# Four terms instead of three in the score products of both attentions

## The chip, the cores and the metric

One of the NeuronCores of one Trainium2 chip runs the whole program as one launch. The metric is the device time of the launch in microseconds (us). Engines in the rows: PE is TensorE (PEld its weight loads), DVE VectorE, ACT ScalarE, POOL GpSimd, SP the engine that here only issues DMAs and waits; a "q" behind an engine's name is its DMA issuing.

## The reference, cut to what matters

Two layers over 4096 tokens of 256 features, 16 heads of 16 features. Layer 0: layer norm, then a sparse attention plus an FP8 product. Layer 1: layer norm, then a causal rotary attention plus a block with its own causal attention (with per-head RMS norms) and a mixture of four experts. All in float32. The scores are what the change touches:

```python
# layer 0: keys of the query's own 128-block, and every 8th key (512 in all)
w = jnp.einsum('bhnqd,bhnkd->bhnqk', fq, fk) * scale + fmask
w = jax.nn.softmax(w, axis=-1)
# layer 1, twice: all earlier keys
scores = jnp.einsum('bhqd,bhkd->bhqk', Q, K) / math.sqrt(Dh)
attn = jax.nn.softmax(jnp.where(causal, scores, min), axis=-1)
```

## The kernel before, in words

Stages run one after another, with a wait of every engine for every queue between them: embed (layer 0's norm and projections), sparse attention, middle (layer 1's projections), dense attention (two attentions, one loop), and a last stage with projections and experts. The function `attend` builds both attention stages.

**Number parts.** A float32 query or key is stored in DRAM as two arrays, its high part (rounded to the format that TensorE takes in one pass) and the low rest. `TERMS` (L27) lists the products that make up a score: high with high, high with low, low with high. Each takes 16 rows (`HEAD_DIM`), so the operand tiles hold 48 rows per head (`TROWS`), and behind them two rows (`MROWS`) that hold ones in the keys and the negated row maximum, in two parts, in the queries: 50 rows (`SROWS`) in all. Two heads lie in one tile, an even one from row 0 and an odd one from row 64 (`HALF`); a tile holds two such pairs side by side. Each term's rows are a DMA of their own: for each of the two halves and three terms, 16 rows of two pieces of 2 KB, 64 KB in all.

**Units.** A unit is one group of 4 heads and one strip of 512 queries: 32 units in the sparse stage, 64 in the dense one (8 groups of 8 strips; strips upwards in even groups, downwards in odd ones). For each unit there are
- "tiles" (L852, L859, L863): score products of queries by keys over `TROWS` rows, of which DVE takes row maxima (L1022, L1026, L1029). Some (L871) go by ACT's copies and POOL's running maximum instead;
- "negate" and "hand": DVE negates the maxima, PE turns them (L876), DVE copies them (L1057), and SP writes them by two DMAs into the spare rows of the query tile (L793);
- "unit", then "score" (L902, L911, L921): score products of keys by queries over `SROWS` rows, so that the maximum is already taken off, and ACT's exponential (L965);
- "weigh" (L942): probabilities by values; "out": PE turns the result, DVE divides, SP stores it (L799).

One list, `order`, fixes the sequence for all engines. The tiles run ahead of the scores, by a distance that starts small in the dense stage and grows with the units done.

**Loads.** SP issues, in the list's order: at first the queries of units 0 and 1 (L754), in the sparse stage with their own keys and values (L763, L765), then the strided keys of three groups (L740), and in the dense stage masks and ones. After that the load of unit n+2 stands at the first tile of unit n+1, and the hand-over of a unit stands behind such a load. A sparse unit is 6 DMAs of queries, 6 of keys and 1 of values. A dense unit is 6 of queries, and in the first 8 units 6 of keys of the first group as well (`load_keys`, L727). The keys of the 7 later dense groups are loaded by POOL, 6 DMAs of 512 KB each and one of values of 2 MB, in two buffers; the load for the second group stands at unit 1. PE waits for counts of these DMAs (`count_loaded`, `handed`, `wait_keys`) at the first tile of a unit and at "unit".

Of the kernel before, what the change touches and what calls it, by code (L numbers as in the profile page):

```python
# [16 lines left out]
P = 128  # L17
# [6 lines left out]
GROUP = 4  # L24
GROUPS = HEADS // GROUP
GCOL = 32
TERMS = ((0, 0), (0, 1), (1, 0))  # L27
TROWS = len(TERMS) * HEAD_DIM
MROWS = 2
SROWS = TROWS + MROWS  # L30
HALF = P // 2
PAIRS = GROUP // 2
SCALE = HEAD_DIM ** -0.5
STRIDE = 8
# [45 lines left out]
def _build(nc, ctx, d, out):  # L80
# [461 lines left out]
    def attend(jobs, stage, splits, past):  # L542
# [4 lines left out]
        held = 6 if sparse else 8  # L547

        per_unit = 16 * 15 if sparse else 16 * 8  # L550
        earlier = 0 if sparse else 4 * 16 * 15

        def count_loaded(n):

            if sparse:
                return per_unit * (n // 8) + 16 * 13
            return earlier + per_unit * (n // 8) + 16 * 12

        def handed(n):

# [111 lines left out]
        with ExitStack() as st:  # L672
# [48 lines left out]
            def load_keys(queue, group, tokens, loaded):  # L721
                a, g = groups[group]
                for odd in range(2):
                    for i, (_, part) in enumerate(TERMS):
                        src = parts_d[a][part][DIM + g * GROUP * HEAD_DIM:DIM + (g + 1) * GROUP * HEAD_DIM, tokens]
                        first_row = odd * HALF + i * HEAD_DIM
                        queue.dma_start(keys[group % 2][first_row:first_row + HEAD_DIM, :, tokens].bitcast(F32),  # L727
                                        src.rearrange("(h o e) t -> o e h t", o=2, e=HEAD_DIM)[odd]).then_inc(loaded, 16)

            def load_values(queue, group):  # L730
                a, g = groups[group]
# [2 lines left out]
            def load_strided(queue, g):  # L734

                for odd in range(2):
                    for i, (_, part) in enumerate(TERMS):
                        src = str_d[part][g * GROUP * HEAD_DIM:(g + 1) * GROUP * HEAD_DIM, :]
                        first_row = odd * HALF + i * HEAD_DIM
                        queue.dma_start(str_keys[g][first_row:first_row + HEAD_DIM, :, :].bitcast(F32),  # L740
                                     src.rearrange("(h o e) t -> o e h t", o=2, e=HEAD_DIM)[odd]).then_inc(str_in[g], 16)
                queue.dma_start(str_values[g][:], v_d[0][g].rearrange("(c p e) n -> p c e n", p=P, e=STRIDE)
                             [:, :, STRIDE - 1, :]).then_inc(str_in[g], 16)

            def attend_sp():
                def load_queries(n):
                    a, g, j = units[n]
                    if n >= held:
                        sp.wait_ge(weighed, ends[n - held])
                    for odd in range(2):  # L750
                        for i, (part, _) in enumerate(TERMS):
                            src = parts_d[a][part][g * GROUP * HEAD_DIM:(g + 1) * GROUP * HEAD_DIM, j * STRIP:(j + 1) * STRIP]
                            first_row = odd * HALF + i * HEAD_DIM
                            sp.dma_start(queries[n % held][first_row:first_row + HEAD_DIM, :, :].bitcast(F32),  # L754
                                         src.rearrange("(h o e) t -> o e h t", o=2, e=HEAD_DIM)[odd]).then_inc(queries_in[n % 8], 16)
                    if not sparse and n < STRIPS:
                        load_keys(sp, 0, slice(j * STRIP, (j + 1) * STRIP), queries_in[n % 8])
                    if sparse:
                        for odd in range(2):
                            for i, (_, part) in enumerate(TERMS):  # L760
                                src = parts_d[a][part][DIM + g * GROUP * HEAD_DIM:DIM + (g + 1) * GROUP * HEAD_DIM, j * STRIP:(j + 1) * STRIP]
                                first_row = odd * HALF + i * HEAD_DIM
                                sp.dma_start(keys[n % held][first_row:first_row + HEAD_DIM, :, :].bitcast(F32),  # L763
                                             src.rearrange("(h o e) t -> o e h t", o=2, e=HEAD_DIM)[odd]).then_inc(queries_in[n % 8], 16)
                        sp.dma_start(values[n % held][:], v_d[a][g, j * STRIP:(j + 1) * STRIP, :].rearrange("(b p) n -> p b n", p=P)).then_inc(queries_in[n % 8], 16)  # L765

                def load_split(i):
                    tiles, loaded, chunks = splits
                    src, high, _ = chunks[i]
                    if i >= 2:  # L770
                        sp.wait_ge(split_done, i - 1)
                    sp.dma_start(tiles[i % 2][:, 0:high.shape[1]], src).then_inc(loaded[i % 2], 16)

                load_queries(0)
                load_queries(1)
                if sparse:
                    for g in range(1, GROUPS):
                        load_strided(sp, g)
                else:
                    for tile, name in halves:  # L780
                        load_halves(tile, name, masks_in)
                    for tile in with_ones:
                        load_ones(sp, tile, masks_in)
                for kind, n, what in order:
                    if kind == "queries" and n + 1 < len(units):
                        load_queries(n + 1)
                    elif kind == "unit" and n < len(splits[2]):
                        load_split(n)
                    elif kind == "hand":
                        sp.wait_ge(side_freed, side_at[kind, n, what] + 1)  # L790
                        for odd in range(2):
                            first_row, rows = odd * HALF + TROWS, MROWS * PAIRS * BLOCKS
                            sp.dma_start(queries[n % held][first_row:first_row + MROWS, :, :].bitcast(F32).rearrange("s h (b p) -> s (h b) p", p=P),  # L793
                                         neg_rows[n % 2][odd * rows:(odd + 1) * rows, :].bitcast(F32)).then_inc(queries_in[n % 8], 16)
                    elif kind == "out":
                        a, g, j = units[n]
                        sp.wait_ge(side_freed, side_at[kind, n, what] + 1)
                        cols = slice(g * GROUP * HEAD_DIM, (g + 1) * GROUP * HEAD_DIM)
                        sp.dma_start(rows_of(ao_d[a], j)[:, :, cols], aos[n % 2][:]).then_inc(ao_stored[n % 2], 16)  # L799

            def wait_keys(n):

                group = n // STRIPS
                if group >= 1:
                    pe.wait_ge(keys_in[group % 2], 96 * ((group + 1) // 2))

            def attend_pe():
                def rows(h, n):
# [23 lines left out]
                for kind, n, what in order:  # L832
# [10 lines left out]
                    if kind == "tile":  # L843
                        kc, h, b = what
                        if what == tiles_of(n)[0]:
                            pe.wait_ge(queries_in[n % 8], count_loaded(n))
                            if sparse:
                                pe.wait_ge(str_in[n // STRIPS], 16 * 7)
                            else:
                                wait_keys(n)  # L850
                        if kc == "strided":
# [1270 lines left out]
```

## Time and profile before

| | |
|---|---|
| median of 3 runs | 5109.05 us |
| lowest, highest | 5077.86, 5117.56 us |
| profiled execution, its own time | 5059.35 us |
| its span | 5057.5 us |
| mean granted TensorE clock in it | 0.931 |
| PE, PEld, DVE, ACT, POOL busy | 92%, 50%, 75%, 61%, 30% |

### The profile page before, as it was taken

How to read it: one execution, taken by the hardware profiler on the slowest of the kernel's cores; microseconds unless marked ns; L12 is line 12 of the kernel's file. 1: busy time of each engine (PE TensorE's matmuls, PEld its weight loads, DVE VectorE, ACT ScalarE, POOL GpSimd, SP SyncE). 2: the span in 40 equal slices, each digit the busy share in tenths (PEclk: the TensorE clock that was granted, in tenths of full speed). 3: DMA queues.
4: the chain of work that ended last, by engine and by line, in shares of the span. 5: the costliest groups of instructions: out<-in, count | busy, mean ns of one | idle time of the engine just before them, and what ended most of it. 6: DMA issues, size and time to landing. Idle time of an engine off the chain costs nothing. (4 is left out here: it accounts for less than half of the span.)

```text
span 5057.5 us, 83460 instructions
## 1 busy us (share of the span) xinstructions
PE 4677.8 (92%) x31872; PEld 2510.8 (50%) x31872; DVE 3799.2 (75%) x8693; ACT 3077.2 (61%) x3565; POOL 1508.0 (30%) x763
## 2 busy tenths in 40 slices
PE   6699997868999999999999999999999998899999
PEld 5455555753433334433334433334433333788888
DVE  8677775766888887888887888887888764555555
ACT  4355554333678776788776788776787876232222
POOL 5200001112465422455432455531455520300000
PEclk9799998876899998999999999999999998899999
DMA  6622223764002001201101201200300000210100
GB/s 191 177 79 67 70 55 107 246 214 92 17 9 31 26 16 32 44 10 23 33 16 23 53 10 15 42 16 19 57 10 6 9 10 6 79 42 22 35 29 9
DMA packets 259192, 258.41 MB, mean 51 GB/s; under 512 B 78288, under 2 KB 198096, under 8 KB 257440
## 3 DMA queue, kind: packets, MB, share of 16 engines
q1 hardware_dynamic: 250784, 212.86, 15.1%
q0 software_dynamic: 6240, 38.80, 4.6%
q8 instruction: 251, 4.11, 0.3%
q10 hardware_dynamic: 1768, 1.42, 0.2%
q14 instruction: 149, 1.22, 0.1%
HBM read 145.44 MB, written 105.97 MB: 50 GB/s over the span
## 5 line engine op out<-in xcount | busy, mean ns | idle before, releaser
L965 ACT ACTIVATE probs_dense<-psum 128x1024 f32<-128x1024 f32 (+3 forms) x2304 | 2078.8, 952 | 638.7 <-PE psum L902 393.3
L1029 DVE TENSOR_REDUCE maxes_dense<-psum 128x1 f32<-128x512 f32 x3152 | 1960.0, 683 | 347.1 <-PE psum L863 344.7
L863 PE MATMUL psum<-keys,queries_dense 48*128 48x512 f32 (+3 forms) x4176 | 1446.0, 459 | 130.3 <-DVE maxes_dense L1022 46.7
L863 PEld LDWEIGHTS psum<-keys,queries_dense 48*128 48x128 f32 x4176 | 651.4, 193 | 1255.3 <-DVE maxes_dense L1029 800.5
L942 PE MATMUL psum<-probs_dense,values 128*32 128x512 f32 (+3 forms) x9216 | 1188.2, 594 | 0.0
L902 PE MATMUL psum<-queries_dense,keys 50*128 50x512 f32 (+3 forms) x4608 | 1082.3, 434 | 35.2 <-ACT probs_dense L965 14.2
L1107 POOL TENSOR_TENSOR max_copies<-max_copies,max_runs 128x1024 f32<-128x1024 f32 x168 | 399.5, 2378 | 1639.1 <-ACT max_copies L982 1639.1
L902 PEld LDWEIGHTS psum<-queries_dense,keys 50*128 50x128 f32 x4608 | 515.3, 194 | 249.2 <-ACT probs_dense L965 104.0
L1022 DVE CUSTOM_DVE_ANT_0 masked_scores_dense<-psum,causal_add 128x128 f32<-128x128 f32 (+3 forms) x1024 | 453.2, 488 | 203.2 <-PE psum L863 195.9
L1109 POOL TENSOR_SCALAR max_copies<-max_copies 128x1024 f32<-128x1024 f32 x168 | 464.7, 2766 | 14.8
L1111 POOL TENSOR_TENSOR max_runs<-max_runs,max_copies 128x1024 f32<-128x1024 f32 x168 | 400.0, 2381 | 14.0
L1022 DVE CUSTOM_DVE_ANT_0 masked_scores_sparse<-psum,after_add 128x512 f32<-128x512 f32 x512 | 326.1, 687 | 90.3 <-PE psum L852 89.2
L1867 ACT ACTIVATE activated<-psum 128x512 f32<-128x512 f32 x208 | 124.3, 598 | 419.0 <-PE psum L76 410.3
L942 PEld LDWEIGHTS psum<-probs_dense,values 128*32 128x32 f32 x9216 | 190.3, 110 | 325.7 <-issue 273.7
L965 ACT ACTIVATE probs_sparse<-psum 128x1024 f32<-128x1024 f32 x224 | 217.3, 1022 | 132.7 <-PE psum L821 51.5
L982 ACT ACTIVATE max_copies<-psum 128x1024 f32<-128x1024 f32 x168 | 172.1, 1024 | 102.5 <-PE psum L871 102.5
L852 PE MATMUL psum<-str_keys,queries_sparse 48*128 48x512 f32 x512 | 177.5, 504 | 50.0 <-DMA own_values<-v_scratch 25.6
L2002 DVE CAST hid_high<-activated 128x512 fp32r<-128x512 f32 x208 | 91.8, 441 | 144.4 <-ACT activated L1867 141.6
L821 PE MATMUL psum<-tri_key,eye_bf 64*128 64x128 bf16 x2048 | 183.8, 228 | 0.0
L871 PE MATMUL psum<-keys,queries_dense 48*128 48x512 f32 x432 | 167.2, 472 | 0.0
L2004 DVE TENSOR_TENSOR hid_low<-activated,hid_high 128x512 fp32r<-128x512 f32 x208 | 148.1, 712 | 7.2
L852 PEld LDWEIGHTS psum<-str_keys,queries_sparse 48*128 48x128 f32 x512 | 70.8, 191 | 165.9 <-DVE maxes_sparse L1022 90.2
(305 smaller groups left out, 5951.6 us busy)
## 6 DMA issues: line engine op xcount, KB each, us to landing
v_scratch<-ve_s SPq DMA_DIRECT2D x96, 256.0 KB, 3.5
queries_dense<-parts_scratch SPq DMA_DIRECT2D x384, 64.0 KB
keys<-parts_scratch POOLq DMA_DIRECT2D x42, 512.0 KB, 18.2
parts_scratch<-part_high SPq DMA_DIRECT2D x16, 1024.0 KB, 4.3
parts_scratch<-part_low SPq DMA_DIRECT2D x16, 1024.0 KB, 7.0
values<-v_scratch POOLq DMA_DIRECT2D x8, 2048.0 KB, 34.9
queries_sparse<-parts_scratch SPq DMA_DIRECT2D x192, 64.0 KB
own_keys<-parts_scratch SPq DMA_DIRECT2D x192, 64.0 KB
```

Source lines behind the costliest of these rows:

```text
L821: m = pe.matmul(bank, eye2[own, part, :], addend, start=start and part == 0, stop=stop and part == 1)
L852: m = pe.matmul(bank, q[rows(h, TROWS), h // 2, b * P:(b + 1) * P], str_keys[n // STRIPS][rows(h, TROWS), h // 2, :], start=True, stop=True)
L863: m = pe.matmul(bank[:, 0:width], q[rows(h, TROWS), h // 2, b * P:(b + 1) * P], k[rows(h, TROWS), h // 2, kc * STRIP:kc * STRIP + width], ...
L902: m = pe.matmul(full[:, first_col:STRIP], k[own, h // 2, c * P:(c + 1) * P], q[own, h // 2, first_col:STRIP], start=True, stop=not diagonal)
L942: m = pe.matmul(psum[own_rows, 4, cols], vt, probs[(2 * m_at + h // 2) % 6][:, h % 2, cols], start=(c == 0), stop=(c == sizes[n] - 1 and b ...
L965: act.activation(probs[i % 6][:, :, first_col:STRIP], psum[:, at2:at2 + 2, first_col:STRIP], ACT.Exp, scale=SCALE, **extra).then_inc(exp_d ...
L982: act.activation(target[:], psum[:, at2:at2 + 2, :], ACT.Copy).then_inc(copied, 1)
L1022: m = dve.tensor_tensor_reduce(out=masked_scores[e % 2][:, 0:width], in0=bank[:, 0:width], in1=mask, scale=1.0, scalar=-3e38, op0=ALU.add, ...
L1029: m = dve.tensor_reduce(mx[:, h * BLOCKS + b, kc:kc + 1], bank, AX.X, ALU.max)
L1107: pool_chain.then(pool.tensor_tensor(copy[:], copy[:], run[:], ALU.subtract))
L1109: pool_chain.then(pool.tensor_scalar(copy[:], copy[:], 0.0, None, ALU.max))
L1111: pool.tensor_tensor(run[:], run[:], copy[:], ALU.add).then_inc(merged, 1)
```

## The change

A fourth term is added: low parts with low parts, of the first 14 of the 16 features, which fills rows 48 to 61 of each half. The two rows of ones and maxima move to rows 62 and 63. `TROWS` goes from 48 to 62 and `SROWS` from 50 to 64. Each place that loads queries or keys issues 8 DMAs instead of 6, the two new ones with 14 rows (56 KB, or 448 KB where POOL loads a whole group's keys). The counts that PE waits for follow.

```diff
-TERMS = ((0, 0), (0, 1), (1, 0))
-TROWS = len(TERMS) * HEAD_DIM
+HALF = P // 2
 MROWS = 2
-SROWS = TROWS + MROWS
-HALF = P // 2
+TROWS = HALF - MROWS
+SROWS = HALF
+TERMS = ((0, 0, HEAD_DIM), (0, 1, HEAD_DIM), (1, 0, HEAD_DIM), (1, 1, TROWS - 3 * HEAD_DIM))
...
-        per_unit = 16 * 15 if sparse else 16 * 8
-        earlier = 0 if sparse else 4 * 16 * 15
+        per_unit = 16 * 19 if sparse else 16 * 10
+        earlier = 0 if sparse else 4 * 16 * 19
...
-                return per_unit * (n // 8) + 16 * 13
-            return earlier + per_unit * (n // 8) + 16 * 12
+                return per_unit * (n // 8) + 16 * 17
+            return earlier + per_unit * (n // 8) + 16 * 16
...
-                    for i, (_, part) in enumerate(TERMS):
+                    for i, (_, part, dims) in enumerate(TERMS):
                         src = parts_d[a][part][DIM + g * GROUP * HEAD_DIM:DIM + (g + 1) * GROUP * HEAD_DIM, tokens]
                         first_row = odd * HALF + i * HEAD_DIM
-                        queue.dma_start(keys[group % 2][first_row:first_row + HEAD_DIM, :, tokens].bitcast(F32),
-                                        src.rearrange("(h o e) t -> o e h t", o=2, e=HEAD_DIM)[odd]).then_inc(loaded, 16)
+                        queue.dma_start(keys[group % 2][first_row:first_row + dims, :, tokens].bitcast(F32),
+                                        src.rearrange("(h o e) t -> o e h t", o=2, e=HEAD_DIM)[odd, 0:dims]).then_inc(loaded, 16)
...
-                    pe.wait_ge(keys_in[group % 2], 96 * ((group + 1) // 2))
+                    pe.wait_ge(keys_in[group % 2], 128 * ((group + 1) // 2))
...
-                                pe.wait_ge(str_in[n // STRIPS], 16 * 7)
+                                pe.wait_ge(str_in[n // STRIPS], 16 * 9)
```

The loads of strided keys, of queries and of a sparse unit's own keys are edited in the same way as `load_keys`.

## Rows read from the trace of the kernel before

**Rows 1.** The page, busy time and instructions by engine, whole span.

```profile
PE 4677.8 (92%) x31872; PEld 2510.8 (50%) x31872; DVE 3799.2 (75%) x8693; ACT 3077.2 (61%) x3565; POOL 1508.0 (30%) x763
```

**Rows 2.** Busy time by stage: length; PE, PEld, DVE, ACT, POOL; clock, DMA share, GB/s.

```profile
222.00:800.00 578.00, 558.47 (x4975) 293.46 (x4975) 431.31 (x1288) 339.21 (x353) 12.86 (x12) 0.97 0.25 63
1126.00:1320.00 194.00, 163.94 (x889) 76.04 (x890) 143.20 (x350) 80.08 (x94) 56.09 (x34) 0.73 0.38 75
1320.00:4260.00 2940.00, 2817.64 (x19596) 1172.52 (x19596) 2410.11 (x5276) 2210.66 (x2455) 1251.34 (x532) 0.96 0.12 22
4360.00:5050.00 690.00, 675.14 (x3787) 590.95 (x3786) 381.57 (x893) 197.24 (x275) 13.77 (x22) 0.96 0.08 26
```

**Rows 3.** Waits, whole span: who waited for whom, us in total, times, longest.

```profile
PEld psum L863 <- DVE maxes_dense L1029: 800.5, 1206, 2.1
PE psum L863 <- DMA queries_dense<-neg_rows_dense: 20.8, 2, 12.2
```

**Rows 4.** Groups by line and form: rows*columns, count, busy us, mean ns, idle before.

```profile
L863 PE MATMUL psum<-keys,queries_dense 48*128 48x512 f32 x3408 | 1264.4, 481 | 63.7 <-DVE maxes_dense L1029 31.9 <-DMA queries_dense<-neg_rows_dense 20.8
L863 PEld LDWEIGHTS psum<-keys,queries_dense 48*128 48x128 f32 x4176 | 651.4, 193 | 1255.3 <-DVE maxes_dense L1029 800.5 <-DVE maxes_dense L1022 254.2 <-issue 96.3
L76 PE MATMUL psum<-hid_high,e_l_high 128*128 128x512 f32 x256 | 102.9, 402 | 0.0
L76 PEld LDWEIGHTS psum<-hid_high,e_l_high 128*128 128x128 f32 x256 | 48.3, 189 | 11.2
```

**Rows 5.** Timeline of SP, start of the sparse stage: start, us, instruction, count.

```profile
178.92 2.66 SPq L754 DMA_DIRECT2D queries_sparse<-parts_scratch  x6
...
217.79 1.51 SPq L793 DMA_DIRECT2D queries_sparse<-neg_rows_sparse  x2
```

**Rows 6.** Timeline of PE, same stretch; in brackets the idle time before.

```profile
221.90 0.80 PE L852 MATMUL psum<-str_keys,queries_sparse 48*128 48x512 f32 x2 [8.64 <-DMA queries_sparse<-neg_rows_sparse]
```

**Rows 7.** Timeline of SP, a usual sparse unit.

```profile
394.36 2.76 SPq L763 DMA_DIRECT2D own_keys<-parts_scratch  x6
397.16 0.43 SPq L765 DMA_DIRECT2D own_values<-v_scratch  x1
400.79 1.28 SPq L793 DMA_DIRECT2D queries_sparse<-neg_rows_sparse  x2
```

**Rows 8.** Busy time in that unit, the stretch in which its load runs.

```profile
392.00:400.00 8.00, 8.00 (x71) 4.29 (x71) 6.65 (x20) 3.88 (x4) 0.00 (x0) 1.00 0.67 147
```

**Rows 9.** Timeline of SP, the sparse unit with the least room ahead of L793.

```profile
525.66 0.42 SPq L765 DMA_DIRECT2D own_values<-v_scratch  x1
527.54 1.28 SPq L793 DMA_DIRECT2D queries_sparse<-neg_rows_sparse  x2
```

**Rows 10.** Timeline of PE in that unit.

```profile
530.19 0.51 PE L852 MATMUL psum<-str_keys,queries_sparse 48*128 48x512 f32 x2
```

**Rows 11.** Waits of SP's queue, whole span.

```profile
SPq L793 <- DVE neg_rows_sparse L1057: 119.9, 31, 12.9
```

**Rows 12.** Timeline of SP, start of the dense stage.

```profile
1117.91 2.67 SPq L754 DMA_DIRECT2D queries_dense<-parts_scratch  x6
...
1145.94 1.40 SPq L793 DMA_DIRECT2D queries_dense<-neg_rows_dense  x2
```

**Rows 13.** Timeline of PE, start of the dense stage.

```profile
1160.51 0.80 PE L863 MATMUL psum<-keys,queries_dense 48*128 48x512 f32 x2 [8.64 <-DMA queries_dense<-neg_rows_dense]
...
1230.93 0.80 PE L863 MATMUL psum<-keys,queries_dense 48*128 48x512 f32 x2 [12.16 <-DMA queries_dense<-neg_rows_dense]
```

**Rows 14.** Timeline of POOL, load of the second dense group's keys.

```profile
1189.91 3.05 POOL L727 DMA_DIRECT2D keys<-parts_scratch  x6
```

**Rows 15.** Busy time from that load to the second of PE's waits.

```profile
1189.90:1230.90 41.00, 27.27 (x163) 11.51 (x155) 24.49 (x55) 11.82 (x15) 12.21 (x10) 0.71 0.99 158
```

**Rows 16.** Busy time in two stretches of the dense stage, at either clock.

```profile
2430.00:2434.00 4.00, 4.00 (x34) 1.58 (x30) 3.50 (x10) 3.27 (x4) 3.91 (x2) 1.00 0.00 0
2440.00:2444.00 4.00, 4.00 (x19) 1.45 (x15) 2.38 (x11) 2.23 (x3) 0.00 (x0) 0.50 0.02 4
```

More of the change, by code:

```diff
@@ L736, in load_strided @@
                 for odd in range(2):
-                    for i, (_, part) in enumerate(TERMS):
+                    for i, (_, part, dims) in enumerate(TERMS):
                         src = str_d[part][g * GROUP * HEAD_DIM:(g + 1) * GROUP * HEAD_DIM, :]
                         first_row = odd * HALF + i * HEAD_DIM
-                        queue.dma_start(str_keys[g][first_row:first_row + HEAD_DIM, :, :].bitcast(F32),
-                                     src.rearrange("(h o e) t -> o e h t", o=2, e=HEAD_DIM)[odd]).then_inc(str_in[g], 16)
+                        queue.dma_start(str_keys[g][first_row:first_row + dims, :, :].bitcast(F32),
+                                     src.rearrange("(h o e) t -> o e h t", o=2, e=HEAD_DIM)[odd, 0:dims]).then_inc(str_in[g], 16)
                 queue.dma_start(str_values[g][:], v_d[0][g].rearrange("(c p e) n -> p c e n", p=P, e=STRIDE)
@@ L750, in load_queries @@
                     for odd in range(2):
-                        for i, (part, _) in enumerate(TERMS):
+                        for i, (part, _, dims) in enumerate(TERMS):
                             src = parts_d[a][part][g * GROUP * HEAD_DIM:(g + 1) * GROUP * HEAD_DIM, j * STRIP:(j + 1) * STRIP]
                             first_row = odd * HALF + i * HEAD_DIM
-                            sp.dma_start(queries[n % held][first_row:first_row + HEAD_DIM, :, :].bitcast(F32),
-                                         src.rearrange("(h o e) t -> o e h t", o=2, e=HEAD_DIM)[odd]).then_inc(queries_in[n % 8], 16)
+                            sp.dma_start(queries[n % held][first_row:first_row + dims, :, :].bitcast(F32),
+                                         src.rearrange("(h o e) t -> o e h t", o=2, e=HEAD_DIM)[odd, 0:dims]).then_inc(queries_in[n % 8], 16)
                     if not sparse and n < STRIPS:
@@ L759, in load_queries @@
                         for odd in range(2):
-                            for i, (_, part) in enumerate(TERMS):
+                            for i, (_, part, dims) in enumerate(TERMS):
                                 src = parts_d[a][part][DIM + g * GROUP * HEAD_DIM:DIM + (g + 1) * GROUP * HEAD_DIM, j * STRIP:(j + 1) * STRIP]
                                 first_row = odd * HALF + i * HEAD_DIM
-                                sp.dma_start(keys[n % held][first_row:first_row + HEAD_DIM, :, :].bitcast(F32),
-                                             src.rearrange("(h o e) t -> o e h t", o=2, e=HEAD_DIM)[odd]).then_inc(queries_in[n % 8], 16)
+                                sp.dma_start(keys[n % held][first_row:first_row + dims, :, :].bitcast(F32),
+                                             src.rearrange("(h o e) t -> o e h t", o=2, e=HEAD_DIM)[odd, 0:dims]).then_inc(queries_in[n % 8], 16)
                         sp.dma_start(values[n % held][:], v_d[a][g, j * STRIP:(j + 1) * STRIP, :].rearrange("(b p) n -> p b n", p=P)).then_inc(queries_in[n % 8], 16)
```

## The prediction, made before the changed kernel was run

> **What bounds the kernel now.** I read the busy shares first, then busy time by stage, the waits, the groups by form, and last the timelines of the places where a wait on a DMA stands. The page alone shows PE at 92% and DVE at 75% [rows 1]. By stage [rows 2] the body of the dense attention, 2940 us, is more than half of the span: PE is busy for 96% of it, DVE for 82%, the DMA engines for 12%. There PE's weight loads wait 800.5 us for DVE's maxima, never longer than 2.1 us [rows 3]: PE and DVE take turns, and neither waits for data. The reader should see two things. The change adds no instruction to PE, DVE or ACT, only rows to operands and DMAs to queues. And DMAs are on the path only where a stage starts: the two waits of PE for the dense hand-over, 20.8 us together [rows 3], both lie in the stage's first 120 us [rows 13], and the sparse stage has one of 8.64 us [rows 6].
>
> **Part 1: more rows in each product, taken as nothing.** 48 rows become 62 in the maxima products and 50 become 64 in the score products. A 512-column product takes 481 ns with 48 rows, at the mix of clocks of the attention, and 402 ns with 128 rows in the last stage; loading 128 weight columns takes 193 ns with 48 rows and 189 with 128 [rows 4]. Neither shows a price per row, and a head still lies within its half of 64. Bounds: nothing below, and nothing above but what rival C says of the clock. DVE and ACT see the same shapes.
>
> **Part 2: the start of the sparse stage, +11 us.** SP issues without a pause from 178.92 to the first hand-over at 217.79 [rows 5]: four units' loads of 13 DMAs and three groups of strided keys and values of 7, 73 DMAs in 38.9 us, 0.53 us each. PE has been idle for 8.64 us when the maxima are in, at 221.90 [rows 6], so the hand-over sets the start. The change adds 4 DMAs to each unit and 2 to each strided group: 4x4 + 3x2 = 22 DMAs, 22 x 0.53 = 11.7 us. At the pace of a quiet queue, 2.76 us for 6 [rows 7], it is 22 x 0.46 = 10.1 us. I take 11; bounds 8 (the added bytes alone, 22 x 57 KB = 1.26 MB at the 158 GB/s of rows 15) and 12. The first tile also comes 2 us later; the same wait covers it.
>
> **Part 3: each later sparse unit, +8 us in all.** The load of a unit, 13 DMAs, stands ahead of a hand-over on SP. Four more at 0.46 us make it 1.9 us longer. What covers them is SP's wait ahead of L793: 119.9 us in 31 waits, 3.9 us in the mean [rows 11]; among the 27 units that matter the least is 527.54 - 526.08 = 1.46 us [rows 9]. If only SP's time counted, four units with less than 1.9 us would lose 1 us in all. But the data counts too: the load runs at 147 GB/s for 8 us, until about 2.4 us after SP has issued it (397.59 to 400.0) [rows 7, 8], and the two DMAs of the maxima queue up behind what is left. In the tightest unit PE went on 2.65 us after the issue (530.19 - 527.54) [rows 9, 10], with no wait to speak of, so 1.46 us of room were enough; whether less is, no row shows. PE has nothing to spare at that point. If 1.46 us is needed, 27 units with 1.9 us less room lose 17 us; if none is, 1 us. I take 8, the middle, since nothing is nearer to one end; bounds 1 and 17.
>
> **Part 4: the start of the dense stage, +8 us.** The same queue: from 1117.91 to the hand-over at 1145.94 [rows 12] SP issues four units of 12 DMAs and 8 DMAs of masks and ones, 56 in 28.0 us, 0.50 each; 4 more for each of four units are 16 x 0.50 = 8.0 us. PE's idle 8.64 us end at 1160.51 [rows 13], 14.6 us after the issue, so transfers in flight (POOL's 2 MB of values among them) hold it too. Those start with unit 1's load, 8 DMAs or 4 us later, and share the engines with three units' added 0.69 MB, 4 us at 158 GB/s: 8 us again. Bounds 4 and 10.
>
> **Part 5: the second dense group's keys, +8 us.** POOL issues 6 DMAs of 512 KB and one of 2 MB at 1189.91 [rows 14]. From there to 1230.9 the DMA engines are 99% busy at 158 GB/s [rows 15], and PE, out of work for 12.16 us, gets the maxima of unit 2 only when that traffic ends [rows 13]. The change adds 2 x 459 KB here and 4 x 57 KB in SP's queue, 1.15 MB: 7.3 us at 158 GB/s. By the six keys' share of the engines' time it is a little more. I take 8; bounds 4 and 12. The other six group loads come where the tiles run up to 36 steps ahead, of 2.6 us each (2940 us over some 1150 steps), and no such wait is in the trace: nothing, and if that cover were gone, at most 8 us each in the three groups that begin with short strips. POOL's 2 more issues at 0.5 us (3.05 for 6) lie in its idle 70% [rows 1].
>
> The Trainium skill ("DMA: Bandwidth & Descriptors", Bandwidth) gives 425 GB/s for one large load and 435 for the ports. By that, part 5's bytes would be 2.7 us and the whole sum an estimated 30 us. The trace speaks for its own rate here, 158 GB/s at a busy share of 0.99 [rows 15].
>
> **Later steps.** The 2 more queries' DMAs of a dense unit, 0.9 us of SP, stand ahead of hand-overs of units whose scores begin many tiles later: nothing. If that cover were gone, 56 x 0.9 = 50 us.
>
> **Sum.** 0 + 11 + 8 + 8 + 8 = 35 us; bounds 17 and 51. Against the profiled execution that is 5059 + 35 = 5094 us. Its time lies 50 us under the median of the runs shown, whose own spread is 40 us, so I set the forecast at the median: 5109 + 35 = 5144 us, +0.7%.
>
> **Rivals.**
> A, the transfers hide (rather less than the sum). For it: stages start with the clock at half and PE waiting for several things, and the waits are put down to the last by the profile. Against it: SP's unbroken issue before both first hand-overs. It would leave part 2 at 8, and the rest at its low ends: 8 + 1 + 4 + 4 = 17 us, 5126.
>
> B, slower. The place is the DMA engines in the sparse stage, between a unit's load and its hand-over. A transfer of 16 rows splits evenly over 16 engines; one of 14 need not. If it lies on half as many, it takes 57 KB / (147/2 GB/s) = 0.8 us instead of 0.4, and the four make a load's tail 1.6 us longer on those engines, on top of the 1.9 us. The mean room of 3.9 us is then 0.4, and against the needed 1.46 the 27 units lose 1.1 us each at the mean and more where the room is small, which units with much room don't give back: some 45 us; with +8 us in each of parts 4 and 5, the sum is 11 + 45 + 16 + 16 = 88 us, 5197. It decides from the point where what is left of a load lasts longer than SP's remaining wait. If they lie on two engines only, the load no longer fits into a unit's 18 us (578 us for 32 units [rows 2]), and it is above 5250.
> The Trainium skill (same page, "Why a DMA increments its semaphore by 16 and not by 1") says that the number of engines is the largest one up to 16 that divides the slowest dimension of both sides. Here that would be 14, two engines idle and no longer transfer, and this rival would fall. No row before shows a 14-row transfer.
>
> C, faster. The clock was 0.73 in the dense stage's first 194 us and 0.96 in its body [rows 2]: half rate for 194 x 0.27 x 2 = 105 and 2940 x 0.04 x 2 = 235 us. At half rate PE began 19 products in 4 us, against 34 [rows 16], so each such us loses 0.44: 150 us in all. If fuller products (62 of 128 rows instead of 48) keep the clock up and half of the body's loss goes, that is -52 + 35 = -17; if all of both goes, 5109 + 35 - 150 = 4994. Against it: the last stage has 128 rows in every product and 98% of PE busy, and its clock is 0.96 too [rows 2].
>
> D, the change does not do what it says. Loads, counts and rows are edited together in all places, so I see no such case.
>
> **How the numbers follow.** A change of this kernel under 1%, 51 us, can't be told from none. Forecast 0.57, A 0.18, B 0.17, C 0.08. The forecast's sum alone is at most 51, but the median of a few runs moves by some 20 us: of its chance 0.14 lies above +1%. With B's 0.15 (the rest of it stays below) that is slower 0.29. Of C, 0.05 is faster, and 0.01 comes from the runs' spread. What is left is 0.65. The range takes in the bounds 17 and 51 with 20 us of spread at either side and B's first value: 5100 to 5197; C, and B with two engines, are left out.
>
> **What would show it.** Right: SP's unbroken issue before the first hand-overs 10 and 8 us longer, the three waits of 8.64, 8.64 and 12.16 us grown, each sparse unit's room 1.9 us less, and the products' means unchanged. Wrong: a mean of L863 or L902 that differs at the same clock; a clock in 1320 to 4260 that isn't 0.96; waits on DMAs in the dense body; a sparse stage more than 30 us longer.

## The result: faster by 1.3%, and the profile after

| | before | after |
|---|---|---|
| median | 5100.44 us (4 runs, 5077.86 to 5117.56) | 5012.09 us (4 runs, 5007.77 to 5017.06) |
| ratio, 95% interval | | 0.9868, 0.9829 to 0.9907 |
| profiled execution, its span | 5059.35, 5057.5 us | 5017.06, 5014.8 us |
| mean granted clock in it | 0.931 | 0.949 |

The changed kernel is 88 us faster at the median, 1.7%. The ratio on record isn't the quotient of the two medians and says 1.3%, so the gain is somewhere from 67 to 88 us. The time is outside the range on record, and what happened is what rival C describes. One run of e8 below, 5498.83 us, counts as slow and is left out of its ratio. The page of the kernel after, busy time by engine:

```profile
PE 4595.3 (92%) x31872; PEld 2471.4 (49%) x31872; DVE 3795.4 (76%) x8693; ACT 3077.2 (61%) x3565; POOL 1515.4 (30%) x777
```

The reader is to see that PE runs the same 31872 products as in [rows 1] in 82.5 us less of busy time, while DVE and ACT stay where they were. The windows of the kernel after, by stage, in the columns of [rows 2]:

```profile
222.00:800.00 578.00, 548.20 (x4975) 289.79 (x4975) 431.08 (x1288) 339.31 (x353) 12.87 (x12) 0.98 0.31 76
1126.00:1320.00 194.00, 148.34 (x808) 69.52 (x808) 133.44 (x334) 75.75 (x87) 57.26 (x36) 0.72 0.47 86
1320.00:4260.00 2940.00, 2798.67 (x19993) 1161.52 (x19992) 2417.66 (x5299) 2239.50 (x2498) 1258.77 (x544) 0.98 0.15 27
4360.00:5010.00 650.00, 639.60 (x3598) 559.10 (x3596) 361.16 (x849) 187.34 (x262) 0.00 (x0) 0.97 0.08 26
...
1190.00:1241.00 51.00, 25.81 (x159) 11.22 (x155) 23.74 (x53) 11.83 (x15) 12.52 (x11) 0.67 1.01 149
```

The body of the dense stage went from clock 0.96 to 0.98, and the same 2940 us hold 19993 products in place of 19596: 2% more work, in 19 us less of busy time. Its groups by line and form (columns as in [rows 4]):

```profile
L863 PE MATMUL psum<-keys,queries_dense 62*128 62x512 f32 x3408 | 1245.9, 471 | 91.4 <-DVE maxes_dense L1029 40.4 <-DMA queries_dense<-neg_rows_dense 36.6
L942 PE MATMUL psum<-probs_dense,values 128*32 128x512 f32 x7680 | 1044.7, 617 | 0.0
L902 PE MATMUL psum<-queries_dense,keys 64*128 64x512 f32 x3840 | 908.8, 444 | 28.0 <-ACT probs_dense L965 11.7 <-ACT max_runs L982 1.6 <-ACT max_copies L982 0.3
L863 PEld LDWEIGHTS psum<-keys,queries_dense 62*128 62x128 f32 x4176 | 636.8, 189 | 1262.6 <-DVE maxes_dense L1029 825.2 <-DVE maxes_dense L1022 256.4 <-issue 61.9
...
L76 PE MATMUL psum<-hid_high,e_l_high 128*128 128x512 f32 x256 | 102.9, 402 | 0.0
```

The two lines of the same view of the kernel before that [rows 4] do not hold:

```profile
L942 PE MATMUL psum<-probs_dense,values 128*32 128x512 f32 x7680 | 1073.4, 632 | 0.0
L902 PE MATMUL psum<-queries_dense,keys 50*128 50x512 f32 x3840 | 928.0, 453 | 28.3 <-ACT probs_dense L965 10.9 <-ACT max_runs L982 3.9
```

Three means fell: L863 from 481 ns [rows 4] to 471, L902 from 453 to 444, and L942, which the change does not touch, from 632 to 617. L76, in the last stage, stands at 402 ns in both. These are means over both clocks. Taken apart, nothing is faster. In a stretch of the dense stage in which the granted clock never falls, 2100 to 2400 us, the kernel before has (its window, then two of its groups there)

```profile
2100.00:2400.00 300.00, 291.84 (x2059) 119.30 (x2051) 259.33 (x514) 241.41 (x266) 163.79 (x72) 1.00 0.09 15
L863 PE MATMUL psum<-keys,queries_dense 48*128 48x512 f32 x371 | 131.9, 457 | 2.5 <-DVE maxes_dense L1029 1.4
L942 PE MATMUL psum<-probs_dense,values 128*32 128x512 f32 x816 | 108.7, 605 | 0.0
```

and the kernel after, in the same stretch,

```profile
2100.00:2400.00 300.00, 291.77 (x2068) 119.11 (x2064) 259.14 (x513) 241.41 (x265) 166.99 (x75) 1.00 0.12 18
L863 PE MATMUL psum<-keys,queries_dense 62*128 62x512 f32 x370 | 131.0, 457 | 2.6 <-DVE maxes_dense L1029 1.4
L942 PE MATMUL psum<-probs_dense,values 128*32 128x512 f32 x824 | 109.7, 605 | 0.0
```

At full clock both kernels begin the same number of products (2059 and 2068) with the same means, at 48 and at 62 rows. At half rate L863 takes 728 ns in both, over the longest spells. What changed is how much of the stage runs at half rate.

One place in the work shows it. [Rows 16] show the kernel before dropping from 1.00 to 0.50 between 2434 and 2440 us. In its timeline of PE this product lies there:

```profile
2438.22 0.32 PE L863 MATMUL psum<-keys,queries_dense 48*128 48x128 f32 x1 [0.73 <-DVE maxes_dense L1022]
```

In the timeline of the kernel after the same product comes 4.9 us earlier, behind the same 0.73 us of idle time (the tiles and weighings of the 25 us ahead of it are in the same sequence in both), and the clock stays at 1.00 there:

```profile
2433.32 0.32 PE L863 MATMUL psum<-keys,queries_dense 62*128 62x128 f32 x1 [0.73 <-DVE maxes_dense L1022]
```

```profile
2435.22:2439.22 4.00, 4.00 (x34) 1.69 (x30) 3.35 (x10) 3.25 (x4) 0.00 (x0) 1.00 0.01 4
2440.00:2444.00 4.00, 3.28 (x21) 1.14 (x18) 3.64 (x7) 2.49 (x3) 0.00 (x0) 1.00 0.00 0
```

The first of them begins 1.9 us behind the product, and the half-rate one of [rows 16] 1.8 us behind its own: 34 products where that had 19. Read in windows of 4 us from 1320 to 4220, the kernel before spends 249 us at half rate in 38 spells, the kernel after 103 us in 21.

What the added DMAs cost, where the prediction looked for it. Timeline of SP, kernel after:

```profile
179.30 3.51 SPq L754 DMA_DIRECT2D queries_sparse<-parts_scratch  x8
...
226.18 1.47 SPq L793 DMA_DIRECT2D queries_sparse<-neg_rows_sparse  x2
...
1116.19 3.52 SPq L754 DMA_DIRECT2D queries_dense<-parts_scratch  x8
...
1154.59 1.40 SPq L793 DMA_DIRECT2D queries_dense<-neg_rows_dense  x2
```

Timeline of PE, kernel after, in brackets the idle time before:

```profile
230.71 0.79 PE L852 MATMUL psum<-str_keys,queries_sparse 62*128 62x512 f32 x2 [12.54 <-DMA queries_sparse<-neg_rows_sparse]
...
1164.79 0.79 PE L863 MATMUL psum<-keys,queries_dense 62*128 62x512 f32 x2 [12.89 <-DMA queries_dense<-neg_rows_dense]
...
1241.27 0.79 PE L863 MATMUL psum<-keys,queries_dense 62*128 62x512 f32 x2 [23.76 <-DMA queries_dense<-neg_rows_dense]
```

Waits of the kernel after, PE's weight loads and SP's queue:

```profile
PEld psum L863 <- DVE maxes_dense L1029: 825.2, 1233, 2.1
...
SPq L793 <- DVE neg_rows_sparse L1057: 67.0, 29, 11.0
```

From SP's first load to PE's going on it was 43.0 us at the sparse start [rows 5, 6] and is 51.4; 42.6 us at the dense start [rows 12, 13] and is 48.6. The wait for the second dense group's keys grew from 12.16 to 23.76 us. Of that, 6 us move the end: between the two wait ends lie 76.5 us, against 70.4. So the three starts cost 8.4 + 6.0 + 6.1 = 20.5 us, where parts 2, 4 and 5 have 27 in their middle and 16 at their low ends, and the clock gave back several times that.

### The profile page after: what moved, and what is told of

Read it like the earlier page. It is cut to its first block and busy times, and to the rows that moved or that the text cites. A ratio compares the mean times of both kernels' runs of the same rounds, so it can differ in the third digit from the quotient of the medians.

```text
span 5014.8 us, 83754 instructions
## 1 busy us (share of the span) xinstructions
PE 4595.3 (92%) x31872; PEld 2471.4 (49%) x31872; DVE 3795.4 (76%) x8693; ACT 3077.2 (61%) x3565; POOL 1515.4 (30%) x777
## 5 line engine op out<-in xcount | busy, mean ns | idle before, releaser
L863 PE MATMUL psum<-keys,queries_dense 62*128 62x512 f32 (+3 forms) x4176 | 1426.2, 450 | 159.6 <-DVE maxes_dense L1022 46.6
L863 PEld LDWEIGHTS psum<-keys,queries_dense 62*128 62x128 f32 x4176 | 636.8, 189 | 1262.6 <-DVE maxes_dense L1029 825.2
L942 PE MATMUL psum<-probs_dense,values 128*32 128x512 f32 (+3 forms) x9216 | 1154.6, 578 | 0.0
L902 PE MATMUL psum<-queries_dense,keys 64*128 64x512 f32 (+3 forms) x4608 | 1059.9, 425 | 34.8 <-ACT probs_dense L965 14.9
L902 PEld LDWEIGHTS psum<-queries_dense,keys 64*128 64x128 f32 x4608 | 498.9, 188 | 244.4 <-ACT probs_dense L965 101.7
L942 PEld LDWEIGHTS psum<-probs_dense,values 128*32 128x32 f32 x9216 | 187.9, 108 | 318.6 <-issue 269.1
L852 PE MATMUL psum<-str_keys,queries_sparse 62*128 62x512 f32 x512 | 177.5, 502 | 58.9 <-DMA own_values<-v_scratch 30.1
L871 PE MATMUL psum<-keys,queries_dense 62*128 62x512 f32 x432 | 161.9, 459 | 0.0
L852 PEld LDWEIGHTS psum<-str_keys,queries_sparse 62*128 62x128 f32 x512 | 70.8, 191 | 175.1 <-DVE maxes_sparse L1022 90.0
```

Of the source, the lines that this page charges most:

```text
L852: m = pe.matmul(bank, q[rows(h, TROWS), h // 2, b * P:(b + 1) * P], str_keys[n // STRIPS][rows(h, TROWS), h // 2, :], start=True, stop=True)
L863: m = pe.matmul(bank[:, 0:width], q[rows(h, TROWS), h // 2, b * P:(b + 1) * P], k[rows(h, TROWS), h // 2, kc * STRIP:kc * STRIP + width], ...
L902: m = pe.matmul(full[:, first_col:STRIP], k[own, h // 2, c * P:(c + 1) * P], q[own, h // 2, first_col:STRIP], start=True, stop=not diagonal)
L942: m = pe.matmul(psum[own_rows, 4, cols], vt, probs[(2 * m_at + h // 2) % 6][:, h % 2, cols], start=(c == 0), stop=(c == sizes[n] - 1 and b ...
```

## The experiments

The runs fall in three sets, each on a chip of its own and with its own runs of the kernel before beside it: medians 5094.67 (13 runs, 5060.93 to 5122.20) for e1 to e4, 5079.55 (14 runs) for e5, e6, e8, e9, and 5078.32 (7 runs) for e7 and e10. Ratios are to the runs of before in the same set; between sets, compare ratios and not medians. The question: do products over more rows keep the clock up (theory R), and if so, which, and do the values in the rows matter (D)? Or was it the added DMAs that shifted the schedule (T)?

**e1: the rows filled once.** Only the first loads into each buffer fill the 14 rows. Later units multiply what is left there, another unit's low parts, so the fourth term is wrong for them; all shapes are those of the kernel after.

```diff
-for i, (part, _, dims) in enumerate(TERMS):
+for i, (part, _, dims) in enumerate(TERMS if n < held else TERMS[:3]):
...
-for i, (_, part, dims) in enumerate(TERMS):            # load_keys
+for i, (_, part, dims) in enumerate(TERMS if group < 2 else TERMS[:3]):
```

> The changed kernel, but the fourth term's 14 rows are loaded only at the first use of each buffer; later units compute with the low parts left over there, so the fourth term belongs to other tokens. 62 and 64 rows in every product, the added DMAs gone from the steady state. Theory R (a product over more rows keeps the clock up): granted clock in the body of the dense stage about 0.98 as in the changed kernel, time 5012 less what the later loads cost, 5000 to 5012. Theory D (it is the values that are added): the same here. Theory T (the added DMAs shift the units against something periodic): like the kernel before, about 5100, body clock 0.957.

Measured: 5002.53 us (5000.81 to 5005.17), ratio 0.9823 (0.9776 to 0.9869), clock 0.952. T fails here already: most of the added DMAs are gone and the gain stays. The time is 10 us under that of the kernel after by the medians. The waits at the starts, where the first loads still fill all rows, are as long as there or nearly (13.07 us in the sparse stage, 20.7 for the second dense group's keys).

**e2: rows of zeros.** As e1, but the 14 rows are filled with zeros from DRAM, so the fourth term adds nothing (`zeros_d` is an array of zeros in DRAM).

```diff
-src.rearrange("(h o e) t -> o e h t", o=2, e=HEAD_DIM)[odd, 0:dims]
+(zeros_d[:, :, slice(0, STRIP)] if i == 3 else src.rearrange("(h o e) t -> o e h t", o=2, e=HEAD_DIM)[odd, 0:dims])
```

> As the run with rows filled once, but the 14 rows hold zeros in queries and keys, so the products have 62 and 64 rows and the sums of three terms, as in the kernel before. Theory R: body clock 0.98 and 5000 to 5012, as with real values. Theory D (rows that carry nothing don't count): body clock 0.957 and about 5100.

Measured: 5021.87 us (5015.89 to 5029.21), ratio 0.9865 (0.9809 to 0.9921), clock 0.949 to 0.952. D falls: rows of zeros hold the clock as well as any, with 86 us at half rate in the dense body (same windows of 4 us) where e1 has 92. The 19 us to e1 are of another kind: the sparse stage is 12 us longer (627.9 against 615.9), with this wait in the timeline of PE of e2:

```profile
238.42 0.79 PE L859 MATMUL psum<-str_keys,queries_sparse 62*128 62x512 f32 x2 [22.71 <-DMA queries_sparse<-neg_rows_sparse]
```

e1 waits 13.07 us there, and e2 has another wait of 1.73 us at 276 us: together 11.4 of the 12 us. All zero fills read the same small array in DRAM; that this makes them slow is the likely reason, and no run takes it alone.

**e3: the DMAs alone.** All 14-row loads of the change, into rows that no product reads (50 to 63); products over 48 and 50 rows. The fourth term is left out.

```diff
-TROWS = HALF - MROWS
-SROWS = HALF
+TROWS = 3 * HEAD_DIM
+SROWS = TROWS + MROWS
...
-first_row = odd * HALF + i * HEAD_DIM
+first_row = odd * HALF + i * HEAD_DIM + (MROWS if i == 3 else 0)
```

> All DMAs of the change, but the low parts go to rows 50 to 63, which no product reads; products have 48 and 50 rows as before, maxima in rows 48 and 49. Theories R and D: clock of the kernel before (0.957 in the body) and its time plus the three longer starts, 5100 + 28 = 5128. Theory T: body clock 0.98 and about 5012.

Measured: 5113.9 us (10 runs, 5089.48 to 5140.83), ratio 1.0038 (1.0007 to 1.0069), clocks 0.918 to 0.931. T falls: with the same DMAs the kernel is 19 us slower than before, not 88 faster. With the DMAs in both, the filled rows are thus worth 1.0038 - 0.9868 = 1.7%, some 86 us, by the ratios; the two medians, of different sets, lie 102 us apart. Windows of e3:

```profile
222.00:800.00 578.00, 552.32 (x4664) 290.94 (x4666) 420.77 (x1254) 316.35 (x329) 12.90 (x12) 0.91 0.29 76
...
1320.00:4220.00 2900.00, 2787.77 (x19227) 1159.53 (x19227) 2379.58 (x5158) 2167.08 (x2406) 1265.55 (x548) 0.95 0.14 27
```

Beside the body's 0.95, the sparse stage stood at 0.91 in this profile, and was 658 us long where the kernel after has 622 and the one before 623. Its wait at the start is 16.94 us, 4.4 more than in the kernel after; most of the rest goes with the clock. The profile is of one of e3's slower runs, 5126.57 us.

**e4: only the score products.** The loads are all there, but the maxima products read 48 rows; score products read 64. The maxima leave out low by low.

```diff
+MAXROWS = 3 * HEAD_DIM
...
-rows(h, TROWS)            # in the products of L852, L859, L863, L871
+rows(h, MAXROWS)
```

> The changed kernel with the maxima products over 48 rows again (the maximum leaves out the low by low products), the score products over 64. Theory R, if every product counts by its rows: about half of the clock's gain, body clock 0.97, 5050 to 5080. If only the score products matter: 5012. If only the maxima products matter: 5120.

Measured: 5025.39 us (5018.66 to 5027.57), ratio 0.9865 (0.9818 to 0.9912), clock 0.944 to 0.947. Against e3, which has the same DMAs and ran on the same chip, filling the 3840 dense score products (and the sparse ones) brings 5113.9 - 5025.4 = 88 us. Filling the maxima products as well brings 13 us more by the medians of e4 and of the kernel after, and nothing by their ratios (0.9865 and 0.9868), which go by different sets: not told from none. I had expected a gain in proportion to the counts, 5050 to 5080: missed. The effect is not one of so much per row and product. No run fills the maxima products alone, with score products over 50 rows, so how much they would bring by themselves isn't shown; only that they add little once the score products are full.

**e5: 56 and 58 rows.** e1 with 8 rows of the fourth term instead of 14 (`TROWS = 56`, `SROWS = TROWS + MROWS`).

> As the run with rows filled once, with 8 rows added instead of 14: maxima products over 56 rows, score products over 58 (the leftover term covers 8 of the 16 features). Theory R by amount (each row counts): about halfway, body clock 0.965 to 0.975, time 5030 to 5060. If only a full half of 64 rows counts (theory F): like the kernel before, body clock 0.957, about 5095. If anything above 50 rows is enough: 5002.

Measured: 5034.1 us (5013.03 to 5043.99), ratio 0.9917 (0.9882 to 0.9952), clocks 0.941 to 0.949. By the ratios that is 0.8% of the 1.8% that e1 brings, and the two intervals don't overlap: about halfway. So it is no rule that wants a full half of 64 rows; and the runs scatter again, 31 us where e1 has 4.

**e8: 40 and 42 rows.** The kernel before with 8 of the 16 features in its third term; the other 8 are left out.

```diff
-TERMS = ((0, 0), (0, 1), (1, 0))
-TROWS = len(TERMS) * HEAD_DIM
+TROWS = 40
+TERMS = ((0, 0, HEAD_DIM), (0, 1, HEAD_DIM), (1, 0, TROWS - 2 * HEAD_DIM))
```

> Fewer rows than before: the third term covers only 8 of the 16 features, maxima products have 40 rows and score products 42, as many DMAs as in the kernel before. Theory R by amount: more half-clock time than before, body clock 0.93 to 0.945, time 5120 to 5160. Theory F, or if rows below 50 make no difference: 5095, body clock 0.957.

Measured: 5441.13 us (5402.18 to 5498.83), ratio 1.0755 (1.0684 to 1.0827), clock 0.831 to 0.853. With less data to move and less to multiply the kernel is 7.5% slower by the ratio (7.1% by the medians). I had expected 5120 to 5160: the direction was right, the size several times too small. It is the strongest sign of the cause. Its page's row of granted clock (40 slices, in tenths), then that of the kernel before:

```profile
PEclk9799878876899975899676899866799987899999
```

```profile
PEclk9799998876899998999999999999999998899999
```

Its groups by form:

```profile
L863 PE MATMUL psum<-keys,queries_dense 40*128 40x512 f32 x3408 | 1351.2, 520 | 50.4 <-DVE maxes_dense L1029 24.0 <-DMA queries_dense<-neg_rows_dense 17.4
L942 PE MATMUL psum<-probs_dense,values 128*32 128x512 f32 x7680 | 1202.5, 703 | 0.0
...
L76 PE MATMUL psum<-hid_high,e_l_high 128*128 128x512 f32 x256 | 102.9, 402 | 0.0
```

The untouched L942 is the meter: 703, 632 and 617 ns at 40, 48 and 62 rows beside it, and L76 stands at 402 ns in all three. Again this is the share of the two clocks and not the price of a product. In a stretch of e8 that stays at full clock, 2250 to 2550 us, the means and the work done are those of the other kernels:

```profile
2250.00:2550.00 300.00, 291.93 (x2066) 119.10 (x2063) 259.38 (x514) 241.50 (x266) 166.15 (x72) 1.00 0.10 16
L863 PE MATMUL psum<-keys,queries_dense 40*128 40x512 f32 x370 | 131.2, 457 | 2.5 <-DVE maxes_dense L1029 1.4
L942 PE MATMUL psum<-probs_dense,values 128*32 128x512 f32 x824 | 109.7, 605 | 0.0
```

The opposite case is the window 1900 to 2100, of e8, then of before, then of after (the same time, not quite the same place in the work):

```profile
1900.00:2100.00 200.00, 191.34 (x1024) 81.57 (x1024) 122.57 (x358) 104.73 (x119) 22.39 (x9) 0.62 0.06 13
```

```profile
1900.00:2100.00 200.00, 190.59 (x1385) 85.61 (x1385) 158.22 (x382) 134.29 (x159) 56.94 (x28) 0.89 0.23 43
```

```profile
1900.00:2100.00 200.00, 186.05 (x1435) 82.20 (x1436) 165.12 (x403) 140.08 (x165) 60.84 (x31) 0.97 0.31 53
```

PE is "busy" for 191, 191 and 186 us; at half rate it counts as busy all the same, and gets less done.

The body of the dense stage from 1320 to 4220 us in the profiled execution of each kernel (of before, e5 and e8 that was one of the fastest runs, of e3 one of the slower), from its windows; the time at half rate is added up from windows of 4 us, and the medians of the launch stand beside it:

| kernel | rows (maxima, score) | clock | at half rate, us | products in 2900 us | median, us |
|---|---|---|---|---|---|
| e8 | 40, 42 | 0.84 | 913 | 17694 | 5441.13 |
| before | 48, 50 | 0.96 | 249 | 19360 | 5079 to 5100 |
| e3 (added DMAs) | 48, 50 | 0.95 | 308 | 19227 | 5113.9 |
| e4 (added DMAs) | 48, 64 | 0.98 | 123 | 19668 | 5025.39 |
| e5 | 56, 58 | 0.98 | 119 | 19623 | 5034.1 |
| e1 | 62, 64 | 0.98 | 92 | 19712 | 5002.53 |
| after (added DMAs) | 62, 64 | 0.98 | 103 | 19676 | 5012.09 |

**e6: the change with its loads moved.** The experiments point at what is left to take: the starts. SP's three groups of strided keys move behind the hand-over of unit 0, and POOL's load of the second dense group from unit 1 to unit 5. All four terms are computed.

```diff
-if sparse: for g in range(1, GROUPS): load_strided(sp, g)              # SP, ahead of the list
+if sparse and n == 0: for g in range(1, GROUPS): load_strided(sp, g)   # SP, behind a hand-over
...
-if not sparse and n == 1:
+if not sparse and n == 5:
-pool.wait_ge(weighed, ends[0])
+pool.wait_ge(weighed, ends[4])
```

> The changed kernel with two loads moved: the strided keys of groups 1 to 3 behind the first hand-over of the sparse stage instead of ahead of it, and POOL's load of the second dense group at unit 5 instead of unit 1. If the three starts are what the added DMAs cost: the waits of 12.5 us (sparse) and 23.8 us (dense) go, time 5012 - 35 = 4977. If the waits only move to another unit: 5012.

Measured: 4985.51 us (4984.45 to 4989.90), ratio 0.9822 (0.9790 to 0.9853). Timeline of PE in e6:

```profile
218.58 0.80 PE L854 MATMUL psum<-str_keys,queries_sparse 62*128 62x512 f32 x2 [2.20 <-DMA queries_sparse<-neg_rows_sparse]
243.68 0.79 PE L854 MATMUL psum<-str_keys,queries_sparse 62*128 62x512 f32 x2 [5.23 <-DMA queries_sparse<-neg_rows_sparse]
...
1158.79 0.80 PE L865 MATMUL psum<-keys,queries_dense 62*128 62x512 f32 x2 [12.87 <-DMA queries_dense<-neg_rows_dense]
```

The sparse wait of 12.54 us is down to 2.20 and a second of 5.23, and the wait of 23.76 us is gone; the dense stage's first wait, 12.87, stays as it was. The body is 24 us shorter than after's (2999.4 against 3023.2, each from 120 us behind the stage's first load to its end), the sparse stage 5 us. By the medians the gain is 27 us of the 35 expected. It is the fastest version that computes everything.

**e9: the same moves on the kernel before.**

> The kernel before, 48 and 50 rows, with only the two loads moved. The waits of 8.6 and 12.2 us at the starts go: 5095 - 20 = 5075, clock as before. If idle time at the starts isn't on the path: 5095.

Measured: 5076.02 us (10 runs, 5047.28 to 5084.19), ratio 0.9985 (0.9960 to 1.0009). The moves that bring some 25 us at 62 rows (27 by the medians, 23 by the ratios) bring nothing to be told from none at 48; the interval reaches down to some 20 us. The expected 5075 was met by luck: it was counted from 5095, and the kernel before ran at 5079.55 in this set. In e9's profile the sparse wait of 8.64 us is down to 2.20 and the one of 12.16 is gone, but its sparse stage is 631.3 us long where before has 623.2, with this window of e9 against the 0.97 of [rows 2]:

```profile
222.00:800.00 578.00, 560.61 (x4871) 294.72 (x4875) 428.55 (x1278) 330.21 (x345) 12.87 (x12) 0.94 0.27 65
```

By these two profiles the clock took back in the sparse stage what the shorter waits gave; why, no run shows.

**e7 and e10: e1 and e2 with the moves.** The fourth term as in e1 and in e2.

> Both together: rows filled at the first use of each buffer (the fourth term of later units belongs to other tokens) and the two loads moved. If the two gains add: 5002 - 27 = 4975 us, body clock 0.98. If they are the same gain: about 4985.

> Rows of zeros, filled at the first use of each buffer, and the two loads moved; the sums are the three terms of the kernel before. If the 19 us by which the rows of zeros were slower than the leftover rows lie in the starts, most of them go with the moved loads: 4975 to 4990. If they lie in the content: 4995.

Measured: e7 4984.72 us (4978.97 to 4989.87), ratio 0.9810 (0.9777 to 0.9843); e10 5001.85 us (4997.51 to 5004.55), ratio 0.9842 (0.9803 to 0.9881). e7 is not measurably faster than e6 (bodies of 2999.3 and 2999.4 us): once the moves are made, the later loads of the fourth term cost nothing that shows. The gains of e1 and of the moves are largely the same gain, as the second expectation of e7 has it. e10 lies 17 us over e7 and meets neither of its expectations. Timeline of PE in e10:

```profile
223.47 0.80 PE L861 MATMUL psum<-str_keys,queries_sparse 62*128 62x512 f32 x2 [6.91 <-DMA queries_sparse<-neg_rows_sparse]
253.46 0.80 PE L861 MATMUL psum<-str_keys,queries_sparse 62*128 62x512 f32 x2 [11.46 <-DMA queries_sparse<-neg_rows_sparse]
```

The same two waits are 2.19 and 3.40 us in e7. So the loads of zeros still hold up the first two hand-overs, by 12.8 us; the sparse stage is 8.7 us longer (625.1 for 616.4) and the body 6.9 (3006.2 for 2999.3), where e10 has 115 us at half rate in its windows and e7 99.

## Why the prediction was wrong, by its steps

**The failed step is Part 1, "more rows in each product, taken as nothing"**, with the argument under rival C that priced it away. Durations per product were right: at full clock L863 takes 457 ns over 40, 48 and 62 rows, so the sign named for a wrong forecast, means that differ at the same clock, did not come; another one named there, a body clock that isn't 0.96, did. What failed was the inference from there to the clock. I took the last stage, 128 rows in every product and a clock of 0.96, as evidence that rows don't matter. It is another stage, with other products and its own pauses, and its clock stays at 0.96 or 0.97 before and after. It could say nothing about the dense body, whose row counts were what changed. What the runs showed in place of a term of nothing: filling the rows takes 146 us of half rate out of 2900 us of the body (before to after) and 1.7% off the launch (e3 to after, same DMAs), and thinning them to 40 adds 664 us of half rate there and 7.5% to the launch. C had the mechanism and a fair price, 0.44 us per microsecond at half rate. By the windows of 4 us, 249 - 103 = 146 us of half rate went; at 0.44 that is 64 us off the body. The body, counted from 120 us behind the stage's first load, became 39.6 us shorter (3062.8 to 3023.2) with 6 + 6 us, or with the whole second wait 6 + 11.6, added at its start: 52 to 57 us, and the rest is within what one profile can tell. Of e8 a somewhat lower price comes out: its body is 284 us longer than that of before (3346.8 us), and over these whole bodies half rate takes 1048 and 283 us, so 0.37 us were lost for each microsecond. C got 0.08. With nothing in the trace that changes rows in the same loop, it deserved a far larger share.

**The base** was also mis-sized for C. The profile of before (5059 us) was one of its fastest runs. Of the 13 in the first set, clock and time go together from 0.933 at 5060.93 us to 0.917 at 5122.20. What a usual run loses to the clock, the profile of its fastest understates. Setting the forecast at the median was right; pricing C from the profile's own half-rate time was not. With fuller products this scatter goes as well: 9 us over four runs, where the kernel before has 40.

**Part 2**, sparse start, +11 us: 8.4 in the profile, at the lower bound. The hand-over was issued 8.0 us later behind SP's first load (46.88 for 38.87), so the 22 DMAs took 0.36 us each and not 0.46 to 0.53. **Part 4**, dense start, +8: 6.0, with a wrong reason. SP's hand-over came 10.4 us later (38.40 for 28.03) and PE only 6.0: what PE waited for there was not the issue alone, and the other transfers in flight, which the part names too, hold it. **Part 5**, second group's keys, +8: the wait grew by 11.6 us, the wait's end came 6 later relative to the first; within its bounds of 4 and 12. The pace there is 149 GB/s, a little under the 158 it was reckoned with. **Part 3**, each later sparse unit, +8: about 1. SP's wait ahead of L793 fell from 119.9 us [rows 11] to 67.0, as said, and PE's waits for hand-overs between 260 and 780 us rose only from 5.7 to 7.2 us. The tail of the load did not need the 1.46 us of room. The whole of the added transfers comes to some 20 to 25 us; e3, which measures them alone at 48 rows, says 19, with an interval of 4 to 35.

**Rival B**, slower, fell. The sparse stage is no longer than before (621.7 us for 623.2), its hand-overs between 260 and 780 us are waited for 1.5 us longer in all, and the 14-row loads are issued at the pace of the 16-row ones: 8 DMAs in 3.51 us, 6 took 2.66 [rows 5]. By the Trainium skill ("DMA: Bandwidth & Descriptors", "Why a DMA increments its semaphore by 16 and not by 1") 14 rows go over 14 engines; that fits, but the trace has no row of the number of engines itself. The Trainium skill (same page, Bandwidth) gives 425 GB/s for one large load; this traffic reached 149 GB/s at a busy share of 1.01. **Rival A** had the transfers nearly right, at 17 us, and the sign of the whole wrong. **Rival D** fell: the rows above have 62 and 64 rows in the products and 8 DMAs in a load.

**What stays open.** The runs show that the granted clock goes with the rows of the products, at equal columns and counts, that filling the score products is enough for nearly all of it, and that zeros count like data. They don't show why: rows from 40 to 64 were tried, the 32 columns of L942's weights and the pauses of PE were not. Filling the maxima products on top of full score products brings little or nothing, which I can't explain, and filling them alone was not run. The thinning of e8 also makes its third term's loads thinner; the DMA engines are 11% busy in its body, so I take that for nothing, but no run separates it. That the sparse stage of e3 falls to 0.91 and that of e9 to 0.94, where the kernel after keeps 0.98, is from one profile each.

## What to carry to other kernels

Read the granted clock by stage, and price its loss at both levels before pricing anything else. If a stage with PE busy all the time has half-rate spells, ask how many rows its products fill: filling them, with zeros if need be, cost PE nothing per product here and was worth 1.7%; thinning them from 48 to 40 rows cost 7.5%. Compare products at one clock before calling them slower: here the same product had one mean at full clock at 40, 48 and 62 rows, and only the share of half rate moved. And don't argue from one stage's clock to another's: a small test that changes only the rows settles it.

## What the hardware showed that was not expected

- In this kernel the granted clock goes with how many of the 128 rows the products use, at nearly the same PE busy share: 0.84, 0.96 and 0.98 in the dense body at 40, 48 and 62 rows. It is steep below 48: 8 rows fewer cost 5441 - 5080 = 361 us, 14 more bring 88.
- Rows of zeros count as rows: the body of e2 has 86 us at half rate, that of e1 92.
- Untouched products are slower in the mean beside thin ones, L942 at 703, 632 and 617 ns, and at full clock it takes 605 ns beside all three.
- Full score products (3840 of 512 columns in the dense stage) are enough: they bring 88 us, and filling the maxima products (3408) on top at most 13 or so.
- A wait that was taken away on thin products (e9) gave nothing to be told from none, and the same one on full products (e6) some 25 us.
